# Cross attention: four of a group's sixteen SBUF moves issued by ScalarE, the other twelve by SyncE in another order

## The reference

```python
x = _layernorm(x + _L0_attn_ref(x, ...))                  # self attention, causal, relu scores times a distance factor
x = _layernorm(x + _L0_xattn_ref(x, ctx_1024, ctx_1024, ...))   # cross attention
x = _layernorm(x + _L0_ffn_ref(x, ...))                   # gated feed forward, width 1536
```

```python
q = (query @ Wq.T + bq);  k = (key @ Wk.T + bk);  v = (value @ Wv.T + bv)      # 16 heads of 32
scores = jnp.einsum('bqhd,bkhd->bhqk', q * scale, k)
probs = jax.nn.softmax(scores, axis=-1)
attn = jnp.einsum('bhqk,bkhd->bqhd', probs, v).reshape(b, lq, HIDDEN)
return attn @ Wo.T + bo
```

## Time and profile before

| | |
|---|---|
| runs, us | 2707.34, 2710.19, 2714.36 (median 2710.19) |
| profiled execution, us | 2718.46, of which the span is 2716.7 |
| PE busy over the span | 2518.8 (93%) |
| DVE, ACT, POOL busy | 1533.1 (56%), 1290.7 (48%), 1344.5 (49%) |
| DMA engines, mean busy share of the cross attention's slices | 0.7 |
| cross attention | from about 597 to about 2164 us of the span |

### The profile page before, as it was taken

One profiled execution on the slowest core, in us unless ns is written; L12 is line 12 of the kernel. 1 busy time (PEld: TensorE's weight loads), 2 busy tenths in 40 slices (PEclk: granted clock), 3 DMA queues, 4 the chain that ended last, 5 costly groups with the idle time before them and its releaser, 6 DMA issues. The chain is left out here.

```text
span 2716.7 us, 56719 instructions
## 1 busy us (share of the span) xinstructions
PE 2518.8 (93%) x21216; PEld 2053.3 (76%) x21216; DVE 1533.1 (56%) x2593; ACT 1290.7 (48%) x2452; POOL 1344.5 (49%) x1185
## 2 busy tenths in 40 slices
PE   8999989979999999999999999999999469999998
PEld 7888857877777777777777777777777268988987
DVE  7555568826566665666666665566666434254242
ACT  4544442125655555566555665565556342312311
POOL 4666553225655555555565555555554223323322
PEclk9999979989999999999999999999999689999999
DMA  7554537526777777777777677776776651011010
GB/s 230 159 151 121 144 115 275 206 87 159 175 177 172 170 178 169 179 174 173 178 173 175 167 177 177 172 178 166 177 177 157 143 201 43 16 59 42 15 35 20
DMA packets 273600, 398.03 MB, mean 147 GB/s; under 512 B 140220, under 2 KB 153532, under 8 KB 273340
## 3 DMA queue, kind: packets, MB, share of 16 engines
q1 hardware_dynamic: 273340, 394.58, 55.5%
HBM read 140.66 MB, written 52.43 MB: 71 GB/s over the span
## 5 line engine op out<-in xcount | busy, mean ns | idle before, releaser
L1098 POOL TENSOR_SCALAR D_e<-D_e,D_inv 128x722 f32<-128x722 f32 x256 | 538.2, 2102 | 676.5 <-DVE D_inv L1187 676.5
L1181 DVE TENSOR_REDUCE D_neg_max<-D_ps_s 128x1 f32<-128x722 f32 x512 | 442.0, 905 | 560.5 <-PE D_ps_s L1255 560.5
L1148 ACT ACTIVATE D_e<-D_ps_s,D_neg_max 128x722 f32<-128x722 f32 x512 | 437.6, 861 | 251.1 <-DVE D_neg_max L1181 251.1
L1195 DVE STREAM_TRANSPOSE D_turned<-D_e 128x768 f32<-128x768 f32 x512 | 483.4, 962 | 1.4 <-POOL D_e L1098 1.3
L65 PE MATMUL D_ps_p<-D_ctx_high,cross_wk_high 128*128 128x362 f32 x1024 | 369.8, 361 | 12.2 <-DVE D_ctx_low L1210 12.2
L65 PE MATMUL D_ps_p<-D_ctx_low,cross_wk_high 128*128 128x362 f32 x1024 | 342.1, 334 | 0.0
L65 PE MATMUL D_ps_p<-D_ctx_high,cross_wk_low 128*128 128x362 f32 x1024 | 340.7, 333 | 0.0
L65 PE MATMUL D_ps_p<-cross_wv_high,D_ctx_high 128*128 128x512 f32 (+1 forms) x768 | 304.2, 396 | 0.0
L65 PE MATMUL D_ps_p<-cross_wv_high,D_ctx_low 128*128 128x512 f32 (+1 forms) x768 | 302.5, 394 | 0.0
L65 PE MATMUL D_ps_p<-cross_wv_low,D_ctx_high 128*128 128x512 f32 (+1 forms) x768 | 302.5, 394 | 0.0
L65 PEld LDWEIGHTS D_ps_p<-D_ctx_high,cross_wk_high 128*128 128x128 f32 x1024 | 196.6, 192 | 96.6 <-issue 96.2
(11 more groups left out here) (187 smaller groups left out, 5050.3 us busy)
## 6 DMA issues: line engine op xcount, KB each, us to landing
D_pT<-D_turned SPq DMA_DIRECT2D x2048, 96.0 KB, 2.2
D_craw<-in_ctxT SPq DMA_DIRECT2D x126, 361.0 KB, 3.8
D_qraw<-cross_q SPq DMA_DIRECT2D x64, 200.0 KB, 3.8
self_q<-A_q_out SPq DMA_DIRECT2D x10, 640.0 KB, 3.7
self_k<-A_k_out SPq DMA_DIRECT2D x10, 640.0 KB, 3.2
self_v<-A_v_out SPq DMA_DIRECT2D x25, 256.0 KB, 2.1
A_q<-self_q SPq DMA_DIRECT2D x32, 200.0 KB, 4.0
A_k<-self_k SPq DMA_DIRECT2D x32, 200.0 KB, 4.5
```

Of the source, the lines that this page charges most:

```text
L1098: pool.tensor_scalar(head, head, inv[:, 2 * (s % 2):2 * (s % 2) + 1], None, ALU.mult)\
L1148: act.activation(e[n // 2 % 2][:, n % 2, 0:S].rearrange("p (a b) -> p a b", a=2), both_banks(n), ACT.Exp, bias=neg_max[:, n % 4:n % 4 + 1] ...
L1181: dve.tensor_reduce(neg_max[:, n % 4:n % 4 + 1], both_banks(n), AX.XY, ALU.max, negate=True)\
L1195: dve.transpose(turned[quad % 2][:, :, 2 * (s % 2) + h, :].rearrange("p j (t r) -> p t j r", r=32), e[s % 2][:, h, :].rearrange("p (t j r) ...
```

## The change

In a group, the four moves with j equal to a (source and destination on the same partitions) leave SyncE. ScalarE issues them in a new function `move_diagonal(s)` at the end of its step: with quad = s // 2 - 1, the blocks 0 and 2 in the even step and the blocks 1 and 3 in the odd step, after the same two waits that SyncE has. Two more rounds of it stand behind the last step. SyncE issues the twelve others, in an order in which the source goes 0, 2, 1, 3 and the distance d from source to destination is 1, then 2, then 3. The count that the weighted sum waits for stays at sixteen DMAs. Apart from that the semaphore `passed` is made once and handed to the three phases (the signatures change, no instruction does).

```diff
                 def move(quad):
                     sp.wait_ge(turn_done, 4 * quad + 4)
                     wait(sp, pv_done, quad - 1)
-                    for j in range(BLOCKS):
-                        for a in range(BLOCKS):
+                    for d in range(1, BLOCKS):
+                        for a in (0, 2, 1, 3):
+                            j = (a + d) % BLOCKS
                             sp.dma_start(pT[quad % 2][32 * j:32 * (j + 1), a, :, :],
                                          turned[quad % 2][32 * a:32 * (a + 1), j, :, :]).then_inc(moved_sem(quad), 16)
...
+                def move_diagonal(s):
+                    quad = s // 2 - 1
+                    act.wait_ge(turn_done, 4 * quad + 4)
+                    wait(act, pv_done, quad - 1)
+                    for a in ((0, 2), (1, 3))[s % 2]:
+                        rows = slice(32 * a, 32 * (a + 1))
+                        act.dma_start(pT[quad % 2][rows, a, :, :], turned[quad % 2][rows, a, :, :])\
+                           .then_inc(moved_sem(quad), 16)
+
...
-                for s in range(FIRST, STEPS):
+                for s in range(FIRST, STEPS + 2):
+                    if s >= STEPS:
+                        move_diagonal(s)
+                        continue
                     if s >= 0:
                         exps(2 * s)
                         exps(2 * s + 1)
...
                     for kind, b, n in unit_at.get(s, []):
                         if kind == "v":
                             take_values(b, n)
+                    if s > 1:
+                        move_diagonal(s)
```

More of the change, by code:

```diff
@@ L146, in split_weights, with phase_self_attention @@
     return load, high, low
-def phase_self_attention(nc, sem, xT, wq, wk, wv, w, v, q_d, k_d, v_d, o_d, x, bo, bq, x1_d, cq_d, raws, cross_w,
+def phase_self_attention(nc, sem, passed, xT, wq, wk, wv, w, v, q_d, k_d, v_d, o_d, x, bo, bq, x1_d, cq_d, raws, cross_w,
                          w_gate, w_up, w_down, biggest):
@@ L286, in phase_self_attention @@
         q_done, qf_done = sem("C_q_done"), sem("C_qf_done")
-        q_stored, passed = sem("C_q_stored"), sem("C_passed")
+        q_stored = sem("C_q_stored")
         int_loaded, int_max = [sem(f"C_int_loaded{j}") for j in range(3)], sem("C_int_max")
@@ L914, in phase_self_attention, with phase_cross_attention @@
     return cross
-def phase_cross_attention(nc, sem, ctxT, cq_d, W, bk, bv, o_d):
+def phase_cross_attention(nc, sem, passed, ctxT, cq_d, W, bk, bv, o_d):
     ST = -(-S // P)
@@ L972, in phase_cross_attention @@
         pv_done, o_done = sem("D_pv_done"), sem("D_o_done")
-        stored, passed = [sem("D_stored0"), sem("D_stored1")], sem("D_passed")
+        stored = [sem("D_stored0"), sem("D_stored1")]
         def both_banks(n):
@@ L1286, in _, with phase_feed_forward @@
                             values_unit(b, n)
-def phase_feed_forward(nc, sem, o_d, x1_d, wo, bo, w_gate, w_up, w_down, biggest, out):
+def phase_feed_forward(nc, sem, passed, o_d, x1_d, wo, bo, w_gate, w_up, w_down, biggest, out):
     PIECES = 3 * KD
@@ L1348, in phase_feed_forward @@
         norm_done = {n: sem("E_norm_" + n) for n in "ab"}
-        stored, passed = [sem("E_stored0"), sem("E_stored1")], sem("E_passed")
+        stored = [sem("E_stored0"), sem("E_stored1")]
         HU = 2 * KF
@@ L1729, in dram @@
             return nc.dram_tensor(name, shape, F32, kind="Internal").ap()
+        passed = sem("passed")
         q_d, k_d, v_d = dram("self_q", [D, N]), dram("self_k", [D, N]), dram("self_v", [N, D])
@@ L1738, in cross_w @@
                 return outer.enter_context(nc.sbuf_tensor(name, shape, dt))
[L1740 to L1743, removed]
+            held = phase_self_attention(nc, sem, passed, xT, a_wq, a_wk, a_wv, a_w, a_v, q_d, k_d, v_d, o_d, x, a_bo,
+                                        x_bq, x1_d, cq_d, (a_wo, x_wq, x_wk, x_wv), cross_w, w_gate, w_up, w_down, biggest)
+            phase_cross_attention(nc, sem, passed, ctxT, cq_d, held, x_bk, x_bv, co_d)
+        phase_feed_forward(nc, sem, passed, co_d, x1_d, x_wo, x_bo, w_gate, w_up, w_down, biggest, out)
 def kernel(x, ctx_1024, L0_attn_Wq, L0_attn_Wk, L0_attn_Wv, L0_attn_Wo, L0_attn_bo, L0_attn_w, L0_attn_v,
```

## The result

| | before | after |
|---|---|---|
| median of the runs, us | 2708.77 (2702.61 to 2714.36) | 2616.18 (2614.92 to 2617.56) |
| profiled execution, us (span) | 2718.46 (2716.7) | 2617.56 (2615.8) |
| PE busy over the span | 93% | 96% |

The ratio is 0.9659, 95% interval 0.9637 to 0.9681: 92.6 us less by the medians. The forecast was 2632 in a range of 2606 to 2697; the time lies 16 us under the forecast and inside the range.

A forecast was written before the change was run, and what follows sets the result against it. SyncE's full issuing queue was taken as the bound, PE second by 5%. Steady waits of 72.3 us plus 10 at the end, less 4 kept, took the profiled 2718.5 to 2640; 8.3 off gave 2632, range 2606 to 2697.

The forecast's parts named there:

- The bound: Cross attention: SyncE's issuing queue, 47.6 us of work in 48.1, paces the phase; PE is second by 5%.
- PE without waits: 45.8 us a sequence: Steady cross attention: without its waits for moves PE would need 45.8 us a sequence instead of 48.2.
- SyncE with twelve, 36.7 us a sequence, 80% full: SyncE's queue: losing 4 of 16 moves a group takes 10.9 us a sequence from 47.6, leaving 36.7.
- ACT's issues: ACT gains two issues a step at 0.64 us each, going from 3.57 to 4.87 us, below PE's 5.73.
- After the short step it is free for only 0.39 us: ACT after the short step: the next exponentials start 0.9 us late, hidden by 2.1 us of cover before the scores.
- ACT's new waits: nothing: ACT's waits for `turn_done` and the weighted sum two groups back hold up no exponentials: cost nothing.
- The margin kept for waits that stay, 4 us: Sequences where ACT's second pair of moves comes late: 4 us of waits kept, between 0 and 20.
- The end of the phase, 10 us: Last four groups, where PE waits 24 us for moves: 10 us saved, between bounds of 5 and 17.
- The steady part, 72.3 us: Cross attention up to 2080 us: PE's waits for the moves, 72.3 us, were counted as saved.
- ACT late: Rival: ACT issues cost 0.9 to 1.1 us or exponentials slip; perhaps half of 72 us returns, 2645 to 2695; chance 0.18.
- One issue path for both: Rival: ACT and SyncE issues can't run side by side, 1.28 us per ACT issue, +27 us, 2737; chance 0.11.
- The transfers pace the phase: Rival: the sixteen moves land no sooner whoever issues them; time stays at 2702 to 2712; chance 0.05.

The follow-up runs named there:

- The added work: Four needless matmuls on PE ahead of each second weighted sum: in the kernel before, ratio 0.9972; in the changed kernel, 0.989 to the kernel before.
- the half bytes: Kernel before with each of the sixteen moves carrying two of the group's four heads, 48 KB instead of 96 KB: ratio 0.9924.
- the later sum: Kernel before with the weighted sum one step later (SUM_AFTER 6 instead of 5): ratio 0.9957.
- the two single edits: Kernel before with SyncE issuing all sixteen moves in the new order: 0.9992; changed kernel with SyncE's twelve moves in the old order: 0.9647.
- four and six a step: Changed kernel with ACT issuing four or six moves a step, SyncE eight or four a group: ratio to the kernel before 0.9778 and 1.052.

## Why the prediction was right, and what it missed

**The bound.** Right. SyncE's full queue was the pace, PE second by 5%. The added work, the half bytes, the later sum and the two single edits all say so.

**PE without waits: 45.8 us a sequence.** 45.45 measured, just below the 45.6 to 46.5 that was named as a sign.

**SyncE with twelve, 36.7 us a sequence, 80% full.** 83% measured; 12 moves take 8.3 to 8.5 us, not 8.1. Landing went from 2.2 to 2.5 us in the median (2.7 for ACT's moves), the few tenths that were allowed for. The reason given there, three moves in flight instead of two, does not fit the rows: with a move every 0.65 us and 2.2 us to its landing, more than three are in flight before the change as well.

**ACT's issues.** The duration was right (median 0.59, as on SyncE in the earlier trace rows; two take 1.18 to 1.28 us). The delay of 0.9 us after the short step did not come: the exponentials there idle for 0.44 us instead of 0.39 in the earlier trace rows. The step that failed is "After the short step it is free for only 0.39 us": the issues do not wait for the activation ahead to end, and 0.84 of their 1.18 us lie under it. The prediction named this as its lower bound and laid the issues end to end behind the activation instead. It cost nothing in the steady part because both readings hid the issues; for four and six a step the same reading gives 6.1 and 7.3 us where 5.8 and 6.6 were measured.

**ACT's new waits: nothing.** Nearly so: in 1000 to 2000 us ACT waited for a weighted sum once, for 1.7 us.

**The margin kept for waits that stay, 4 us.** None stayed; up to the sum of group 123 PE has no wait for moves.

**The end of the phase, 10 us.** 7.8 measured, between the bounds of 5 and 17. The last two sums still wait 6.8 and 5.5 us. ACT's issues are not free there: the view puts the idle time ahead of the exponentials at 2036.58 and at 2041.69 to "issue", 0.58 and 0.56 us, and they start 0.11 us after the second issue. What that costs at the end no run shows.

**The steady part, 72.3 us.** 96.9 measured; this is the term that was too small, by 24.6 us. 3.9 of them are two waits, before the sums of groups 121 (0.78) and 123 (3.07), which lay behind the 2080 us up to which the waits were added up. The larger part is the clock. The prediction took a wait of PE to cost its own length; it put the slower clock at some 15 us, but used that for the low end of the range alone. These rows of the kernel before show a wait of 2.61 us and what followed; the windows give the granted clock last but two:

```profile
1098.42 0.89 PE L1255 MATMUL D_ps_s<-D_keys,D_queries 32*128 32x361 f32 x8
1101.92 2.23 PE L1271 MATMUL D_ps_p<-D_pT,D_values 128*32 128x100 f32 x48 [2.61 <-DMA D_pT<-D_turned]
1104.07 0.67 PE L65 MATMUL D_ps_p<-D_ctx_high,cross_wk_high 128*128 128x362 f32 x1
...
1099.00:1101.00 2.00, 0.30 (x5) 0.00 (x0) 1.63 (x2) 0.80 (x2) 0.00 (x0) 1.00 0.66 154
1101.50:1104.50 3.00, 2.58 (x49) 2.29 (x50) 0.29 (x2) 0.61 (x2) 0.00 (x0) 0.50 0.96 299
1105.00:1109.00 4.00, 4.00 (x21) 3.12 (x21) 1.38 (x4) 1.35 (x2) 2.32 (x2) 1.00 0.62 135
```

The sum takes 2.23 us at a granted clock of 0.50 instead of 1.26 at 1.00, and the first keys matmul behind it 0.67 instead of 0.43. Other falls lie in the units behind a sum. What they cost together is seen in PE's busy time from the first sum to that of group 123, in which PE does the same matmuls in each of these kernels (13024; the edge of the last window takes in one more): before, with the new order alone, with half the bytes, and changed.

```profile
624.72:2118.82 1494.10, 1417.51 (x13024) 1093.37 (x13020) 914.59 (x1601) 888.70 (x1663) 849.25 (x731) 0.99 0.72 173
```

```profile
627.77:2108.67 1480.90, 1407.64 (x13024) 1083.47 (x13020) 914.55 (x1601) 888.96 (x1663) 849.18 (x731) 1.00 0.70 174
```

```profile
627.19:2087.55 1460.36, 1401.02 (x13024) 1077.76 (x13020) 914.19 (x1601) 888.59 (x1662) 849.24 (x731) 1.00 0.43 110
```

```profile
629.02:2026.25 1397.23, 1397.23 (x13025) 1077.62 (x13021) 908.28 (x1599) 888.81 (x1658) 849.34 (x731) 1.00 0.71 184
```

PE waits 76.2 us in the first of these stretches and is busy 20.3 us longer than in the last: with that the 96.9 us are found but for 0.4. The trace says where the 20 us lie. In ten places, 37.5 us together, the granted clock is 0.50. Take the time from one sum to the next, less the wait, and compare it with the same interval after the change: the intervals with a slow place take 16.4 us more, the other intervals with a wait 3.7 us more (0.07 each), and the rest 0.6. The other two kernels agree. With the new order alone there are nearly as many waits (72.8 us) but four slow places, 13.7 us together, which cost 6.3 us; with half the bytes there is none before the sum of group 123 and PE is busy only 4 us longer than after the change, although it waits 59 us.

So a wait costs its length, a few hundredths of a us more, and what the slower clock takes if it follows. How often it follows differs from execution to execution: over the runs of the kernel before, the mean granted clock of the whole span goes from 0.967 to 0.974, and the runs with the lower clock are mostly the longer ones. The profiled execution, with 0.968, lies 9.7 us above the median of its runs. With the needless matmuls in its waits the kernel before has no slow place ahead of the sum of group 123, and yet its time fell by 7.5 us only: SyncE's queue was still the pace.

**Why the sum came so near.** For the profiled executions 2640 was forecast and 2617.6 measured, 22.6 us apart: 24.6 of the steady part, 4 of the margin and 0.5 behind the cross attention, against 2.2 that the end of the phase gave less and 4.3 of the later start. Against the medians only 16 are left, since the 8.3 us by which the profiled execution was above its median were taken off. That the start came later is luck.

**The rivals.** *ACT late* did not come at two a step; it comes at four. *One issue path for both* did not come: SyncE's issues keep a median of 594 ns with ACT issuing beside them (592 before), the longest 2.02 us in 1000 to 2000 (2.03 before), and ACT's have 592 over the phase. The exclusive lock that the Trainium skill describes (Perfetto Trace Analysis, section DMA Instruction — HWDGE (DVE, Sync)) costs nothing that shows in these rows. *The transfers pace the phase* fell with the half bytes. The Trainium skill's rule that a second issuing engine saves only sequencer time, which it calls usually small beside the DMA (DMA: Bandwidth & Descriptors, section Issuing engines are not separate DMA queues), agrees with the runs as to what is saved. It was not small here: an issue takes 0.59 us beside 2.2 us to its landing, and 64 of them a sequence filled the queue and were the bound.

No version tried was measurably faster than the changed kernel.

## What to carry to other kernels

When one queue issues many small DMAs, add up its own timeline over a period of the kernel and compare the sum with the period; where they are equal, that sequencer is the pace even if another engine is busy 95% of the time, and moving a few issues elsewhere is enough (two of sixteen did here). Work added into an engine's waits tells whether it is the pace: it is free where the engine isn't. And a wait of PE may cost more than its length: look at the granted clock behind it, and compare PE's busy time for the same matmuls in two kernels.

## What the runs showed that was not expected

- An issue on ACT starts 0.06 us after the activation ahead has started; with four a step 0.54 of 2.51 us of issuing were hidden that way. Two a step were free, four cost 0.13 us a step, six 0.96.
- After PE had idled for 2.6 us the granted clock was 0.50 for some 3 us (1.2 GHz, where 1.00 is 2.4 GHz), while after the wait of 0.16 us in the earlier trace rows the sum took its normal 1.26 us. The length of the wait alone does not tell: of the 19 waits of 1.75 us and more before group 123, ten were followed by such a stretch and nine, one of 2.42 us among them, were not. Some 70 us of needless matmuls, half of the sums having them ahead, made the kernel 0.28% faster.
- A move of half the bytes takes just as long to issue (0.591 us) and lands only 0.2 us sooner.
